# Second attention of a four-layer kernel: keys split and stored ahead, parts of a row side by side, seven packs a unit

## The reference

```python
def _L1_xattn_ref(q, k, v, gamma):          # q = normalised x, k = v = ctx_2048; (8, 128, 256) each
    h, dq = 8, 16                           # 8 heads of 16 rows, 256 columns are the positions
    scale = 1.0 / sqrt(dq)
    qk = einsum('bhdq,bhdl->bhql', qh, kh) * scale
    sm = softmax(qk, axis=-1)
    ret = einsum('bhql,bhdl->bhdq', sm, vh)
    return gamma * ret.reshape(B, Dv, Lq)
```

## Time and profile before

| | us |
|---|---|
| three runs | 1244.24, 1250.89, 1250.78 (median 1250.78) |
| the profiled execution | 1240.12 |
| its span, first to last instruction | 1238.3 |
| expert stage, from the barrier to the last expert's result | 183 to 299 |
| second attention, from the first gather to the last `x` | 301 to 431 |
| mean granted TensorE clock over the span | 0.875 of full |

### The profile page before, as it was taken

One profiled execution on the slowest core, in us unless ns is written; L12 is line 12 of the kernel. 1 busy time (PEld: TensorE's weight loads), 2 busy tenths in 40 slices (PEclk: granted clock), 3 DMA queues, 4 the chain that ended last, 5 costly groups with the idle time before them and its releaser, 6 DMA issues.

```text
span 1238.3 us, 18952 instructions
## 1 busy us (share of the span) xinstructions
PE 960.1 (78%) x6616; PEld 565.7 (46%) x6616; DVE 655.5 (53%) x1548; ACT 438.1 (35%) x721; POOL 388.8 (31%) x527
## 2 busy tenths in 40 slices
PE   4899975885288799577648953898989999279993
PEld 1455544775044345456425741243434444246562
DVE  5778734342567513278662436978778781311111
ACT  1466651110044421155311420075646667012220
POOL 5223202122854000334213015165555656200002
PEclk9999996888578899899768985599999999689997
DMA  6344514654433000544233833101030000810002
GB/s 179 113 120 152 179 48 162 204 189 153 111 97 103 22 26 0 161 95 93 62 147 108 254 120 89 39 2 39 3 135 9 1 3 6 321 48 22 17 14 77
DMA packets 117437, 115.29 MB, mean 93 GB/s; under 512 B 71752, under 2 KB 107144, under 8 KB 114312
## 3 DMA queue, kind: packets, MB, share of 16 engines
q1 hardware_dynamic: 106496, 95.58, 25.0%
q10 hardware_dynamic: 7776, 10.10, 2.6%
q0 software_dynamic: 3072, 8.39, 2.2%
HBM read 88.17 MB, written 29.62 MB: 95 GB/s over the span
## 4 chain that ended last, share of the span: by engine, by line
PE 47%; DVE 15%; issue 7%; DMA 5%; POOL 5%; ACT 2%; SPq 2%; another core or an unknown queue 1%; POOLq 0%; DVEq 0%; ACTq 0%
PE psT L1123 7%; PE psT L1422 6%; PE psT L1274 5%; DVE mxp L1813 4%; PE psB L1238 4%; PE psB L1123 3%; PE psB L1436 3%; PE psO L1318 3%; PE psB L1487 2%; PE psT L1385 2%; PE psB L1463 2%; PE psO L1308 2%; PE psO L1306 2%; DVE mxp L1817 1%; SPq L2259 1%
## 5 line engine op out<-in xcount | busy, mean ns | idle before, releaser
L1813 DVE TENSOR_REDUCE mxp<-psB 128x1 f32<-128x512 f32 x256 | 163.0, 684 | 38.5 <-PE psB L1238 37.3
L1274 PE MATMUL psT<-whole 99*128 99x256 bf16 (+2 forms) x1024 | 156.2, 279 | 14.6 <-issue 8.2
L1817 DVE TENSOR_REDUCE mxp<-psB 128x2 f32<-128x512 f32 x192 | 122.1, 684 | 34.5 <-PE psB L1244 34.0
L1573 ACT ACTIVATE Pt<-psT,ln 128x1024 f32<-128x1024 f32 x96 | 106.4, 1113 | 63.7 <-PE psT L1274 62.8
L1274 PEld LDWEIGHTS psT<-whole 99*128 99x128 bf16 (+2 forms) x1024 | 96.8, 102 | 63.8 <-issue 32.1
L1573 ACT ACTIVATE Pt<-psT 128x1024 f32<-128x1024 f32 x96 | 98.1, 1024 | 59.3 <-PE psT L1274 57.3
L1244 PE MATMUL psB<-whole 96*128 96x256 bf16 x384 | 77.8, 315 | 52.4 <-issue 46.7
L1238 PE MATMUL psB<-whole 96*128 96x512 bf16 x256 | 97.3, 429 | 26.1 <-DMA whole<-scr_q 13.8
L2144 POOL TENSOR_TENSOR rstd<-vare,cst 128x1 f32<-128x1 f32 x64 | 35.8, 580 | 260.2 <-DVE vare L1731 260.0
L1422 PE MATMUL psT<-whole,qf 128*128 x176 | 80.7, 602 | 0.6 <-ACT qf L1622 0.6
L2201 POOL TENSOR_SCALAR nb_t<-Pt 128x1024 f16<-128x1024 f32 x64 | 66.8, 1044 | 37.4 <-ACT Pt L1573 35.3
(11 more groups left out here) (308 smaller groups left out, 1764.5 us busy)
## 6 DMA issues: line engine op xcount, KB each, us to landing
whole<-in_w SPq DMA_DIRECT2D x32, 512.0 KB, 4.7
whole<-in_w SPq DMA_DIRECT2D x5, 3072.0 KB, 10.3
xn<-scr_sorted ACTq DMA_DIRECT2D x42, 128.0 KB, 2.2
scr_q<-sq SPq DMA_DIRECT2D x48, 96.0 KB, 1.9
scr_k<-sk SPq DMA_DIRECT2D x48, 96.0 KB, 1.9
whole<-scr_k SPq DMA_DIRECT2D x24, 192.0 KB, 3.4
whole<-scr_k SPq DMA_DIRECT2D x72, 64.0 KB, 3.5
whole<-scr_q SPq DMA_DIRECT2D x64, 64.0 KB
```

Source lines behind the costliest of these rows:

```text
L1274: ins = pe.matmul(psT[:, s.n % 2, i * A.T:(i + 1) * A.T], lhsT=k_at[:, h * kw + s.c * P:h * kw + (s.c + 1) * P], rhs=q_at[:, h * A.T:(h + ...
L1573: act.activation(p_slot(A, s.p)[:, 0:4 * A.T], psT[:, s.n % 2, 0:4 * A.T], ACT.Exp, bias=bias).then_inc(T_used[s.n % 2], 1)
L1813: dve.tensor_reduce(mxp[:, s.un.g % 2, at:at + 1], psB[:, s.n % BANKS, :], AX.X, ALU.max).then_inc(bank_used[s.n % BANKS], 1)
L1817: dve.tensor_reduce(mxp[:, s.un.g % 2, at:at + 2], psB[:, s.n % BANKS, :].rearrange("p (h n) -> p h n", h=2), AX.X, ALU.max).then_inc(bank ...
```

## The change

1. The keys of the second attention are split (on POOL) and stored (by SP) in `moe_capacity`: batches 0 to 3 (`KEYS1_FIRST`) after the weight loads and before the routing, batches 4 to 7 after the scatters and before the loads of the experts' tokens. They go to `scr_k1_all` (three parts side by side, one DMA per batch) and once more, high and middle parts alone, to `scr_k1_high` (one DMA).
2. In the second attention only queries are split, straight from `xn`; the factor 0.25 becomes the scale of the exponential. They are stored with their three parts side by side, in two DMAs of 64 rows.
3. With parts side by side (row d, part c) is one stride, so the packs of a unit are three for keys (48, 32 and 16 rows) and four for queries (48, 16, 16, 16 rows) in place of six and six. The key packs are a step of their own, `packk`: for units 0 and 1 at the beginning of the attention, for the others just ahead of `packs`.
4. The due times of all four attentions are changed. In the second: packs 1.343 to 1.608, max_first 1.89 to 2.13, max_end 2.607 to 2.713, neg 2.791 to 2.846, span 0.983 to 0.958. In the others the shifts are up to 0.2 of a period.

```diff
+KEYS1_FIRST = 4
 TIMES = [
-    dict(front=0.339, store=0.638, packs=0.799, max=1.019, max_end=1.768, neg=1.872, body=2.312, end=3.927, start=0.37, span=1.018, max_first=1.418),
-    dict(front=0.315, store=0.667, packs=1.343, max=1.871, max_end=2.607, neg=2.791, body=3.334, end=5.361, start=0.069, span=0.983, max_first=1.89),
...
+    dict(front=0.339, store=0.638, packs=0.793, max=1.019, max_end=1.817, neg=1.926, body=2.312, end=3.927, start=0.17, span=1.026, max_first=1.418),
+    dict(front=0.315, store=0.667, packs=1.608, max=1.871, max_end=2.713, neg=2.846, body=3.334, end=5.364, start=0, span=0.958, max_first=2.13),
...
+    def keys1_ahead(batches):
+
+        for u in batches:
+            keys1[u] = Record(A=ATT[1], u=u, k=take("k"))
+            add("split", un=keys1[u], A=ATT[1], kind_of="k1")
+            add("store", un=keys1[u], A=ATT[1], kind_of="k1")
...
         add("attn_begin", A=A)
+        if A.layer == 1:
+            for u in range(2):
+                add("packk", un=Record(A=A, u=u, g=n["unit"] + u, k=keys1[u].k), A=A, done_before=-1)
...
             def packs():
+                if A.layer == 1 and u >= 2:
+                    add("packk", un=r, A=A, done_before=done())
                 add("packs", un=r, A=A, done_before=done())
...
             eload(e, 1)
+        keys1_ahead(range(KEYS1_FIRST))
         route(0, take("M"))
         v_last = values_ahead()
         for b in range(NB):
             add("scatter", b=b)
+        keys1_ahead(range(KEYS1_FIRST, NB))
...
+                        if A.layer == 1:
+                            for m in range(2):
+                                rows_ = slice(m * 64, (m + 1) * 64)
+                                sp.dma_start(by_row(dq[u.g % 2])[rows_], sq[rows_, u.g % 2, :, 0:256]
+                                             ).then_inc(q_stored[u.g % 2], 16)
...
+                    if s.kind_of == "k1":
+                        sp.wait_ge(parts_k, u.k + 1)
+                        sp.dma_start(dk1[u.u], sk[:, u.k % 2, :, 0:256]).then_inc(k_stored[u.k % 2], 16)
+                        sp.dma_start(dk1_high[u.u], sk[:, u.k % 2, 0:2, 0:256]).then_inc(k_stored[u.k % 2], 16)
...
+                elif s.kind == "packk":
+                    A, u = s.A, s.un
+                    if s.done_before >= 0:
+                        sp.wait_ge(PV_done, s.done_before + 1)
+                    sp.wait_ge(k_stored[u.k % 2], 32 * (u.k // 2 + 1))
+                    slot, done = KP[:, 4096 * (u.g % 3):4096 * (u.g % 3 + 1)], k_packed[u.g % 2]
+                    sp.dma_start(heads(slot, 0, 2, 48), dk1[u.u].rearrange("(h d) c n -> (d c) h n", h=A.H)).then_inc(done, 16)
+                    sp.dma_start(heads(slot, 33, 2, 32), dk1_high[u.u].rearrange("(h d) c n -> (d c) h n", h=A.H)
+                                 ).then_inc(done, 16)
+                    sp.dma_start(heads(slot, 1, 2, 16), dk1[u.u][:, 0].rearrange("(h d) n -> d h n", h=A.H)).then_inc(done, 16)
...
+                    if A.layer == 1:
+                        slot, done, src = QP[:, u.g % 3, :], q_packed[u.g % 2], by_row(dq[u.g % 2])
+                        sp.dma_start(heads(slot, 0, 2, 48), src.rearrange("(h d) c n -> (d c) h n", h=A.H)).then_inc(done, 16)
+                        for c in range(2):
+                            sp.dma_start(heads(slot, 33 + 2 * c, 4, 16), src[:, 1 + c].rearrange("(h d) n -> d h n", h=A.H)
+                                         ).then_inc(done, 16)
+                        sp.dma_start(heads(slot, 1, 2, 16), src[:, 2].rearrange("(h d) n -> d h n", h=A.H)).then_inc(done, 16)
...
-                        act.activation(p_slot(A, s.p)[:, 0:4 * A.T], psT[:, s.n % 2, 0:4 * A.T], ACT.Exp, bias=bias
+                        scale = float(A.d) ** -0.5 if A.layer == 1 else 1.0
+                        act.activation(p_slot(A, s.p)[:, 0:4 * A.T], psT[:, s.n % 2, 0:4 * A.T], ACT.Exp, bias=bias,
+                                       scale=scale
...
-                            link(pool.tensor_scalar(qf[:, u.g % 2, 0:256], xn[:, u.u, :], 0.25, 0.0, ALU.mult, ALU.add))
```

More of the change, by code:

```diff
@@ L141 @@
 TIMES = [
-    dict(front=0.339, store=0.638, packs=0.799, max=1.019, max_end=1.768, neg=1.872, body=2.312, end=3.927, start=0.37, span=1.018, max_first=1.418),
-    dict(front=0.315, store=0.667, packs=1.343, max=1.871, max_end=2.607, neg=2.791, body=3.334, end=5.361, start=0.069, span=0.983, max_first=1.89),
-    dict(front=0.498, fronts=[-0.15, 0.1, 0.25, 0.35, 0.45], store=0.58, packs=0.683, body=1.604, end=3.227, start=0.084, span=1.053),
-    dict(front=0.077, fronts=[0.0, 0.005, 0.01, 0.02, 0.03, 0.04, 0.045, 0.045, 0.045, 0.045, 0.045, 0.058, 0.06, 0.079],
-         rest=[0.0, 0.02, 0.06, 0.08, 0.11, 0.13, 0.15, 0.18, 0.21, 0.24, 0.27, 0.33, 0.34, 0.35], store=0.42, packs=0.43, max=1.011, max_end=1.919, neg=2.006, body=1.639, end=3.415, start=0, span=1.008, max_first=1.026)]
+    dict(front=0.339, store=0.638, packs=0.793, max=1.019, max_end=1.817, neg=1.926, body=2.312, end=3.927, start=0.17, span=1.026, max_first=1.418),
+    dict(front=0.315, store=0.667, packs=1.608, max=1.871, max_end=2.713, neg=2.846, body=3.334, end=5.364, start=0, span=0.958, max_first=2.13),
+    dict(front=0.368, fronts=[-0.15, 0.1, 0.278, 0.262, 0.45], store=0.58, packs=0.684, body=1.604, end=3.227, start=0.084, span=1.053),
+    dict(front=0, fronts=[0.0, 0.005, 0.01, 0.02, 0.03, 0.04, 0.045, 0.045, 0.045, 0.045, 0.045, 0.058, 0.06, 0.079], rest=[0.0, 0.02, 0.06, 0.08, 0.11, 0.13, 0.15, 0.18, 0.21, 0.24, 0.27, 0.33, 0.34, 0.35], store=0.42, packs=0.43, max=0.909, max_end=1.919, neg=1.973, body=1.639, end=3.415, start=0, span=1.008, max_first=1.026)]
 def plan():
@@ L250, in front @@
             b0 = u * A.nb
-            r = Record(A=A, b0=b0, u=u, g=take("unit"), k=take("k") if A.layer < 3 else None)
+            k = None if A.layer == 3 else keys1[u].k if A.layer == 1 else take("k")
+            r = Record(A=A, b0=b0, u=u, g=take("unit"), k=k)
             units.append(r)
-            r.packed_before = packed[r.g % 2]
-            packed[r.g % 2] += 16 * (6 if A.layer == 1 else 3)
-            r.packed = packed[r.g % 2]
+            r.packed_before, r.k_packed_before = list(packed[r.g % 2])
+            packed[r.g % 2][0] += 16 * (4 if A.layer == 1 else 3)
+            packed[r.g % 2][1] += 16 * 3
+            r.packed, r.k_packed = packed[r.g % 2]
             def fn(j):
@@ L309, in split @@
             def split():
[L310 removed]
+                add("split", un=r, A=A, kind_of="q" if A.layer == 1 else "qk")
             def store():
[L313 removed]
+                add("store", un=r, A=A, kind_of="q" if A.layer == 1 else "qk")
             def packs():
+                if A.layer == 1 and u >= 2:
+                    add("packk", un=r, A=A, done_before=done())
                 add("packs", un=r, A=A, done_before=done())
@@ L2163, in _ @@
                         pool.wait_ge(parts_k, 1)
-                    elif u.k is not None:
+                    elif s.kind_of != "q" and u.k is not None:
                         if A.layer != 1:
@@ L2251, in pack @@
         c0 = first if is_q else 0
-        if A.layer == 1:
-            for c in range(n):
-                rows = dst[at + c:96:6, 0:A.H * width].rearrange("r (h n) -> r h n", h=A.H)
-                sp.dma_start(rows, src[c0 + c, :, 0:width].rearrange("(h d) n -> d h n", d=A.d)).then_inc(sem, 16)
-        else:
-            begin, step = ((0, 4), (33, 4), (66, 4))[first] if A.layer == 0 else ((0, 2), (33, 2), (1, 2))[first]
-            rows = dst[begin:begin + (n * A.d - 1) * step + 1:step, 0:A.H * width].rearrange("r (h n) -> r h n", h=A.H)
-            sp.dma_start(rows[:, h0:h1, :], src[c0:c0 + n, :, 0:width].rearrange("c (d h) n -> (c d) h n", d=A.d)[:, h0:h1, :]
-                         ).then_inc(sem, 16)
-        at += n
+        begin, step = ((0, 4), (33, 4), (66, 4))[first] if A.layer == 0 else ((0, 2), (33, 2), (1, 2))[first]
+        rows = dst[begin:begin + (n * A.d - 1) * step + 1:step, 0:A.H * width].rearrange("r (h n) -> r h n", h=A.H)
+        sp.dma_start(rows[:, h0:h1, :], src[c0:c0 + n, :, 0:width].rearrange("c (d h) n -> (c d) h n", d=A.d)[:, h0:h1, :]
+                     ).then_inc(sem, 16)
 def kernel(**inputs):
```

33 lines of the change are left out of this document (20 added, 13 removed).

## The result

The changed kernel took 1230.84 us (median of four executions, 1229.19 to 1233.8). Its time ratio to the kernel before is **0.9869**, with a 95% interval of 0.9835 to 0.9903: some 16 us faster by the ratio (19 by the medians of the same batch, 1249.96 and 1230.84), where -6.9 us had been predicted, and the time lies under the predicted range of 1234 to 1256 us. Its profiled execution took 1231.18 us, with a span of 1229.4 us; that of before had 1240.12 us. So the two traces differ by 8.9 us and the timed runs by 16 by their ratio. Both numbers have to be explained.

The account below looks back on a forecast made before the run. SP's never idle issue queue was taken to bound the second attention, with PE left little idle elsewhere. Expert stage +16.3, second attention -23.2, rest 0: -6.9 us from 1250.8 gives 1243.9 us, range 1234 to 1256.

Parts of the forecast that it names:

- The expert stage: Expert stage: key splits and stores around the scatters delay expert 0's tokens, 6.5 us ahead and 9.8 behind, +16.3 us.
- Rival B: Expert stage: key stores not held up by the weights, only 9.8 us lost; -13.4 us, 1237.4 us, chance 0.15.
- The fill of the second attention: Second attention's start: fewer packs bring the first smax to 322.0 from 327.30 us; -7.2 us by unit 2.
- The 1 us that I took for gathers: Second attention's start: early key packs hold up the first gathers by 1 us, between 0 and 2.9.
- Its steady part: Second attention, units 2 to 7: PE and DVE bound at 9.1 us a unit for 11.91; 14.1 us go.
- Rival C: Second attention: every second unit still falls to the lower clock, 10.9 us a unit; +2.1 us, 1252.9 us, chance 0.18.
- D: Second attention: clock stays at half throughout, 12.2 us a unit; +10.6 us, 1261.4 us, chance 0.10.
- The rest: Exponential's scale, copy of values and the other attentions' new due times: 0 us, between -6 and +4.
- Rival E: Other attentions: due times worth 6 us to either side, 1238 or 1250 us; chance 0.11 gain, 0.04 loss.
- The carry-over: Whole kernel: the difference from the profiled 1240.12 us applied to the runs' median, 1250.8 - 6.9 = 1243.9 us.

Follow-up runs that it names:

- E4: The changed kernel with the key splits and stores of batches 0 and 1 ahead of the weight loads of experts 2 and 3; ratio to before 0.9846.
- E10: The changed kernel with the key splits and stores of batches 4 to 7 moved from behind the scatters to between the first experts; ratio to before 0.981.
- E8: The changed kernel with the second attention's packs cut back to 16 rows, six and six a unit, keys still split ahead; ratio to before 0.9999.
- E2: The changed kernel with the old due times in the first, third and fourth attention; ratio to before 0.9943.
- E9: The kernel before with only the new due times of the first, third and fourth attention; ratio to before 0.9936.
- E1: The kernel before, unchanged, run once more; ratio to before 1.0007, profiled execution with a span of 1246.8 us.
- E12: The kernel before with only the new due times of the third attention; ratio to before 1.0001.
- E3: The changed kernel with all eight key splits and their stores moved to the end of the first attention; 1215.24 us, ratio to before 0.976.

## Why the prediction was wrong, point by point

**The expert stage (+16.3 us predicted, +17.8 measured** to the last expert's result): right in every step to within 1 us. Third split 196.7 predicted, 196.49 us measured; scatters 201.8 and 201.71; tokens' loads 223.6 and 224.09; PE 225.8 and 226.62. The first attention had ended 1.0 us earlier than in before, which makes up most of the other 1.5 us. E4 shows the wait behind the weights and E10 the 10 us behind the scatters. Rival B, stores not held by the weights, is refuted.

**The fill of the second attention (first `smax` 5.3 us earlier predicted, 6.7 measured).** The 1 us that I took for gathers held up by the key packs did not come: from the first gather to the first `rstd` of the attention it takes 7.3 us, where before had 7.75.

**Its steady part (9.1 us a unit predicted, 8.7 measured).** I had taken PE's work of a unit with its gaps, and even these shrank: PE now fits 8.15 us of work into 8.70. Five units make 2 us. No unit of the steady part falls to half clock (0.50 from 337.4 to 347.0 us, while PE comes out of its long idle, and 1.00 in every unit from 357.66 us on), so rivals C and D are refuted. Rival C rested on a misreading: it took the slow unit of rows 2 for one without a wait for packs, but PE had waited 2.63 us just ahead of it. In before the waits of 2.64, 2.63 and 3.20 us were each followed by a slow unit (clock 0.72, 0.58 and 0.70), the wait of 1.43 us was not (1.00).

```profile
385.64 0.60 PE L1244 MATMUL psB<-whole 96*128 96x256 bf16 x4 [2.63 <-issue]
```

In sum the attention gives -27.1 us (mean of two traces each) where -23.2 was predicted: -8.6 up to the third unit (predicted -7.2), -16.2 in the five units behind it (-14.1), -2.3 in the last (-1.9). The largest cause was right, as E8 shows, and the term was 4 us too small.

These two terms alone are E2: 0.9943 makes -7.1 us (-3.9 to -10.2), where -6.9 was predicted. That the sum fits so well is in part luck, since by the traces both terms were too small and their errors, +1.5 and -3.9 us, partly cancel.

**"The rest. ... I take 0, between -6 and +4": this is the step that failed.** It is -8 us (5 to 11) by E9, and E2 says the same from the other side. I had shown that PE idles little in these attentions and took the shifts for small; I could not read their worth from the trace, and the range I gave reached only to -6. PE's idle time was also the wrong measure of what there was to gain: where the gain can be placed, in the fourth attention, 2.7 of 3.3 us came out of PE's busy time, by the clock, and only 0.6 out of its idle time. Rival E's gain side, which I gave 0.11, came true, and on top of a term that was too small. I had also counted it as an alternative to the forecast, though it adds to every other case. +17.8 - 27.1 - 8 = -17.3 us, against -16.4 by the ratio.

**The carry-over.** I set the difference of two profiled executions against the median of three runs. With -8 for the rest the sum would have given 1250.8 - 17.3 = 1233.5 us, 3 over the measured median; the medians of before in larger batches, 1246 to 1249, show that the three first runs lay high. The profiled execution of before lay low, by 8.5 us against E1's, 5.0 of them in the third attention with its clock (E1), and that is why the two traces differ by only 8.9 us.

What stays open: where 5 of the 8 us of the due times lie, and by what way a shift of due times betters the clock. The traces show 3 us in the fourth attention (7 by the timed runs, uncertain by 5), 1.6 us ahead of the third that E12's timed runs can't confirm, and the first can't be told from its own spread. What makes up the 10 us that the second attention gains without fewer packs (E8) is not taken apart either.

## What to carry to other kernels

Count the issues of a DMA queue per unit of work before its bytes: here seven larger packs in place of twelve took a quarter off each unit of a stage in which all engines had room (11.5 to 8.7 us, E8 against the changed kernel), and the low clock that had followed the three longest waits for them went too. Work moved "ahead" must be laid where its engine, its queue and its buffers are free at once: the same eight splits cost 18 us around the scatters and next to nothing at the end of the attention before. When a change comes with a retuned table, give that table a term of its own, add it to every case, and take its bounds from what executions of one kernel differ by, not from how small the shifts look.

## What the runs showed of the hardware

**POOL slows DVE.** From `xn` to the last index of the routing DVE takes 11.4 and 11.5 us in before and E3, 12.1 us in the changed kernel (two splits beside it) and 13.4 us in E4 (four splits beside it). Single operations with two inputs on 128x64 grow from 0.22 to 0.45 us, the seven additions from 1.37 to 2.31 us. A reduction, which has one input, does not grow; two neighbours in the changed kernel's trace, beside the second split:

```profile
185.82 0.45 DVE L1765 TENSOR_TENSOR Pt<-Pt,cst 128x64 f32<-128x64 f32 x1
186.31 0.22 DVE L1766 TENSOR_REDUCE r<-Pt 128x8 f32<-128x64 f32 x1
```

The Trainium skill, "SBUF — State Buffer", section "SBUF: two separate sides", says that GpSimd and a DVE operation that has two inputs from SBUF, or runs in a 2-port performance mode, share a port pair under an exclusive lock, so that the loser waits for a whole instruction. The trace agrees for the additions, which have two such inputs, and a split's operation takes 0.41 or 0.67 us. It also shows `L1978`, a TENSOR_SCALAR with one tensor input, at 0.59 us in E4 where the same statement has 0.23 in E3; whether it ran in such a mode no trace here shows.

**Issuing a DMA took longer behind large loads.** The second store pair behind the eight weight loads took SP 1.32 and 3.24 us to issue (1.25 and 3.24 in E10), where the same instructions take 0.51 and 0.63 us with nothing ahead. I had costed issues at a constant price.

**One program, two clocks.** Two executions that agree to 0.4 us for 523 us then had a granted clock of 0.92 and 0.77 in the same 25 us of the third attention, and 5 us between them at its end. A single trace of such a stage is no better than that.
